# Reordering in the state-space stage: the squares of C on GpSimd, a table load on ScalarE, the mask on VectorE

## The reference, cut to what matters

```python
xp = x @ Wx.T                                    # 64 heads of 8
Bm = rmsnorm((x @ WB.T).reshape(B_, L, H, N), Bn_w) + B_bias      # N = 128 per head
Cm = rmsnorm((x @ WC.T).reshape(B_, L, H, N), Cn_w) + C_bias
dt = softplus(x @ Wdt.T); lam = sigmoid(x @ Wlam.T)
theta_cumsum = cumsum(theta * dt[..., None], axis=1)
Bm, Cm = rope(Bm, theta_cumsum), rope(Cm, theta_cumsum)
alpha = exp(dt * A); beta = (1 - lam) * dt * alpha; gamma = lam * dt
# per token: h = alpha * h + beta * (B_prev x_prev) + gamma * (B x);  y = C . h
```

## Time and profile before

| | us |
|---|---|
| median of three executions | 7745.34 (7743.88 to 7745.35) |
| the profiled execution | 7747.07 |
| its span | 7745.3 |
| mean granted TensorE clock | 0.863 of full |

### The profile page before, as it was taken

The page is one execution under the profiler, slowest core; times in us unless marked ns, Lnnn a source line. Parts: engine busy times, 40 slices in busy tenths (PEclk is TensorE's granted clock), DMA queues, the critical chain, the costliest instruction groups (busy, mean ns, idle before and its releaser), DMA issues. The chain is left out here.

```text
span 7745.3 us, 137299 instructions
## 1 busy us (share of the span) xinstructions
PE 6985.7 (90%) x43387; PEld 5087.3 (66%) x43660; DVE 4741.5 (61%) x8121; ACT 3713.1 (48%) x5855; POOL 3482.4 (45%) x3893
## 2 busy tenths in 40 slices
PE   6999999999684699999999999999999999997499
PEld 4777777777573566666666666666666666666287
DVE  4333333333555477777777777777777777772433
ACT  2222222222222366666666666666666666662111
POOL 0000000000000477777777777777777777771000
PEclk8555555555796899999999999999999999998699
DMA  1000000000101211111111111111111111112100
GB/s 47 4 9 1 4 9 4 9 4 1 57 22 49 89 27 29 28 27 27 28 29 27 30 27 27 29 27 30 27 28 27 27 29 29 29 27 95 53 22 16
DMA packets 388293, 214.26 MB, mean 28 GB/s; under 512 B 248036, under 2 KB 343076, under 8 KB 387140
## 3 DMA queue, kind: packets, MB, share of 16 engines
q1 hardware_dynamic: 379588, 203.05, 10.1%
q10 hardware_dynamic: 8448, 8.39, 0.3%
HBM read 162.02 MB, written 40.64 MB: 26 GB/s over the span
## 5 line engine op out<-in xcount | busy, mean ns | idle before, releaser
L1117 POOL MEMSET ss_rot<- 128x4096 f32 x1 | 3.5, 3511 | 2500.9 <-POOLq L1815 2500.9
L1350 ACT ACTIVATE ss_r<-ss_pssum,ss_eps 128x512 f32<-128x512 f32 x512 | 352.5, 688 | 1131.1 <-PE ss_pssum L1280 1131.1
L1280 PE MATMUL ss_pssum<-ss_sq,ss_pairssum 128*128 128x512 f32 x1024 | 595.4, 664 | 184.0 <-POOL ss_sq L1171 181.2
L1159 POOL TENSOR_TENSOR ss_sq<-ss_sq 128x512 f32<-128x512 f32 x256 | 329.6, 1288 | 914.9 <-ACT ss_sq L1359 914.9
L1409 DVE SCALAR_TENSOR_TENSOR ss_psb<-ss_psb,ss_norm,ss_r 128x512 f32<-128x512 f32 x512 | 362.9, 755 | 510.3 <-ACT ss_r L1352 510.3
L329 PE MATMUL a_ps_o<-a_probt,a_vhead 128*128 128x128 f32 x2560 | 639.7, 414 | 3.6 <-issue 3.5
L329 PEld LDWEIGHTS a_ps_o<-a_probt,a_vhead 128*128 128x128 f32 x2560 | 604.5, 330 | 4.0 <-ACT a_probt L383 1.6
L1261 PE MATMUL ss_psse<-ss_rot 64*128 64x128 f32 x8224 | 530.0, 279 | 0.3 <-POOL ss_rot L1144 0.3
L427 DVE TENSOR_REDUCE a_nmax<-a_ps_p 128x1 f32<-128x384 f32 (+1 forms) x256 | 159.9, 625 | 598.7 <-PE a_ps_p L305 598.7
L1192 POOL TENSOR_TENSOR ss_own<-ident,ss_tk 128x512 f32<-128x512 f32 x512 | 524.9, 1048 | 0.0
L48 PE MATMUL ss_psb<-x_hi,ss_whi 128*128 x1024 | 515.3, 503 | 6.7 <-DVE ss_fr L1397 4.5
(11 more groups left out here) (339 smaller groups left out, 18260.8 us busy)
## 6 DMA issues: line engine op xcount, KB each, us to landing
ss_dtb<-time_steps SPq DMA_DIRECT2D x516, 128.0 KB, 2.9
ss_wraw<-in_w_state SPq DMA_DIRECT2D x264, 80.0 KB, 2.4
ss_xp<-x_heads SPq DMA_DIRECT2D x33, 256.0 KB, 4.4
y_heads<-ss_yo SPq DMA_DIRECT2D x132, 64.0 KB, 2.4
x_heads<-xp_outt SPq DMA_DIRECT2D x32, 256.0 KB, 2.0
ss_right<-decay_rows SPq DMA_DIRECT2D x512, 3.0 KB
ss_left<-decay_rows SPq DMA_DIRECT2D x512, 3.0 KB
op_y<-y_heads SPq DMA_DIRECT2D x8, 1024.0 KB, 6.8
```

The costliest lines, as they stand in the source:

```text
L1159: G.tensor_tensor(sq[:, 0, 0], sq[:, 0, 0], sq[:, 0, 1], ALU.add).then_inc(ss_b, 1)
L1280: M(p_sum[:], pairs_sum[:], sq[:, q, 0], start=True, stop=True).then_inc((sum_b, sum_c)[q], 1)
L1350: A(r[:, q], p_sum[:], ACT.Ln, scale=1.0 / N1, bias=eps[:, 0:1]).then_inc(ln, 1)
```

## The change

Three edits, all inside `state_space`. On GpSimd `decays` takes a second argument; for the units of the loop it now adds the squares of C between its two halves, so L1171 runs behind L1149 and ahead of L1150. On ScalarE the load of the logarithm's set moves from the end of `angles` to behind the Square of B. On VectorE `masked(k)` moves from behind `states` into it, between the copy of the first state (L1421) and the update of the second (L1422); the wait for the copy stands behind the mask. A unit computes with the same instructions as before.

```diff
--- before.py
+++ after.py
@@ -1143,10 +1143,13 @@
                 G.tensor_tensor(rot[:, 1 - j, 2], rot[:, 1 - j, 2], tmp[:, 1, 0], ALU.add)
                 G.tensor_tensor(rot[:, 1 - j, 3], rot[:, 1 - j, 3], tmp[:, 1, 1], ALU.add).then_inc(rot_c, 1)
 
-            def decays(k):
+            def decays(k, squares_c):
                 pool.wait_ge(d_done, k + 1)
                 pool.wait_ge(own_done, k)
                 G.tensor_tensor(dec[:, 0:TPB], dec[:, 0:TPB], own[:, 0:TPB], ALU.add)
+                if squares_c:
+                    pool.wait_ge(sq_c, k + 1)
+                    G.tensor_tensor(sq[:, 1, 0], sq[:, 1, 0], sq[:, 1, 1], ALU.add).then_inc(ss_c, 1)
                 G.tensor_tensor(dec[:, TPB:2 * TPB], dec[:, TPB:2 * TPB], own[:, TPB:2 * TPB], ALU.add).then_inc(dd_done, 1)
 
             with pool.Fori(0, UNITS // 2) as n:
@@ -1165,10 +1168,7 @@
                     G.tensor_tensor(w_lo[:, ds(1 - par, 1), :, ds(b * WCH, WCH)], w_raw[:, j:j + 1],
                                     w_hi[:, ds(1 - par, 1), :, ds(b * WCH, WCH)].bitcast(FP32), ALU.subtract)\
                      .then_inc(w_split, 1)
-                    decays(k)
-
-                    pool.wait_ge(sq_c, k + 1)
-                    G.tensor_tensor(sq[:, 1, 0], sq[:, 1, 0], sq[:, 1, 1], ALU.add).then_inc(ss_c, 1)
+                    decays(k, True)
 
                     pool.wait_ge(pair_in[0], (pair // 2 + 1) * 96)
                     pool.wait_ge(pair_in[1], ((pair + 1) // 2) * 96)
@@ -1194,7 +1194,7 @@
                                                at_diagonal[:, h].broadcast_to([P, TPB, P]), ALU.mult)
                     last.then_inc(own_done, 1)
             turned_c(UNITS, 0)
-            decays(UNITS)
+            decays(UNITS, False)
 
         @block.tensor
         def _(pe):
@@ -1332,7 +1332,6 @@
                 A(trig[:, j, 2], fr[:], ACT.Sin, scale=-UNDER_TURN)
                 act.wait_ge(abs_done, count)
                 A(trig[:, j, 1], trig[:, j, 1], ACT.Sin, bias=quarter[:, 0:1], scale=-UNDER_TURN).then_inc(trig_done, 1)
-                nc.scalar.preload_act_table_set("natural_log_exp_and_others")
 
             def decays(k):
                 act.wait_ge(e_done, k + 1)
@@ -1357,6 +1356,7 @@
                     k = n * 2 + j
                     act.wait_ge(b_done, k + 1)
                     A(sq[:, 0], p_b[:], ACT.Square).then_inc(sq_b, 1)
+                    nc.scalar.preload_act_table_set("natural_log_exp_and_others")
                     decays(k)
                     take_b(k, j, 0)
                     norms(k, 0)
@@ -1418,7 +1418,10 @@
                 sums = p_m[:, 0:6 * PW].rearrange("p (g d) -> p g d", d=PW)
                 link(V.tensor_tensor(sums, sums, blocks[:].rearrange("p (o d) -> p o d", o=1).broadcast_to([P, 6, PW]), ALU.mult))
                 entering = lambda c: state[:, c, :, 0:PW]
-                link(V.tensor_copy(entering(1), added[:, 0]))
+                link.mark(V.tensor_copy(entering(1), added[:, 0]))
+                moved = link.n
+                masked(k)
+                link.wait(moved)
                 link(S(entering(2), entering(1), ends[:, ds(at + 1, 1)], added[:, 1], ALU.mult, ALU.add))
                 S(entering(3), entering(2), ends[:, ds(at + 2, 1)], added[:, 2], ALU.mult, ALU.add).then_inc(s_ready, 1)
 
@@ -1442,13 +1445,11 @@
                     combine(k, j, (older // BATCH) % 2, older % BATCH, link)
                     rotate(k, j, k // BATCH, 0, link)
                     states(k, ends_at(old, 1 - j), link)
-                    masked(k)
                     rotate(k, j, k // BATCH, 1, link)
             assert link.n == PER + 1, link.n
             link = Chain(dve, chain_sem, UNITS * (PER + 1) + first)
             combine(UNITS, 0, 1, BATCH - 2, link)
             states(UNITS, ends_at(LAST, 1), link)
-            masked(UNITS)
             combine(UNITS + 1, 1, 1, BATCH - 1, link)
 
 E1, I1 = 8, 176
```

## The result

The changed kernel takes 7466.12 us (median of four, 7463.08 to 7469.45) against 7745.35: a ratio of 0.964, 95% interval 0.9623 to 0.9656. The span of its profiled execution is 7467.7 us.

What follows compares the result with a forecast made beforehand. The loop through GpSimd's squares of C (L1171) was taken to bound the state-space unit. Removing 181.2 us of TensorE waits and 36.1 us of clock falls, 217.3 us together, from 7745.3 gave 7528 us, range 7500 to 7610.

Steps and rivals of the forecast that it cites:

- The covers: Slack hiding moved work: 0.35 us for ScalarE's table load; VectorE's 0.60 us idle ahead of L1422 for the mask.
- the floor: TensorE's own work in one state-space unit, claimed as 16.22 us, the least a unit could take after the change.
- The 36.1 us: State-space stage: time lost to some 22 falls of TensorE's granted clock to half, all forecast to go.
- The 181.2 us: TensorE's total idle time ahead of L1280, waiting for GpSimd's squares of C (L1171), all forecast to go.
- the sum of 217.3 us: Whole forecast gain in the state-space stage: 181.2 us of waits for L1171 plus 36.1 us of clock falls.
- the first rival: TensorE's clock falls stay although the wait goes: 7564 us with 22 falls, 7600 with 44; chance 0.17.
- The mask edit: Masking between VectorE's state updates, claimed to fill its 0.60 us idle time and be worth 0 within 0.1 us.
- The load on TensorE's path (2): Rival: the moved ScalarE load needs over 1.28 us, delaying the copy of B and C projection: 7766 us; chance 0.05.
- The Square is served by the sine's table (3): Rival claimed the opposite: ScalarE's Square of B needs another load ahead of it, giving 7666 us; chance 0.06.
- VectorE (4): Rival: the 0.60 us ahead of L1422 isn't hidden under the mask, TensorE loses up to 0.4 us: 7630; chance 0.08.
- No change (5): Rival: an unseen wait takes the place of the old one, leaving the time as before; chance 0.03.
- The estimate of 7791 us: Kernel time if the moved ScalarE load also cost the skill page's drain of about 1380 ns, a unit taking 17.25 us.

Runs made afterwards that it cites:

- the last run: The changed kernel with two products of three in the angles' projection and only the first half of the mask computed: 7439.06 us, ratio 0.9601.

## Why the prediction was wrong, point by point

- **The mechanism held.** The loop over GpSimd's squares of C bounded the unit, each of load and order removes that wait, their gains don't add, and TensorE is what is left, in the kernel with all three edits. The covers were found where I named them: 0.30 us behind the moved load, and the mask in the place of the 0.60 us.
- **The step that failed is the floor: "TensorE's own work is thus 16.20 us, 16.22 with the 0.02 us seen at a handover".** It is 15.97 us. Of the 0.25 us, 0.15 us is the end of the chunk sums: I took it from a row's start and length, and the next product starts 0.15 us before it. Nearly all of the other 0.1 us (0.09 us between the rows of one unit, 0.08 us by the run without the load edit) is a wait for L1159, the squares of B, inside the unit that I took as free of waits. I had treated 4392.73 as TensorE's own pace, since no wait was shown on it; the load edit removes this one too. 0.25 us in 255 units are 64 us, and the forecast missed by 62.
- **The falls of the clock.** The 36.1 us are TensorE's extra time at half the clock, and as that they are right: the trace's record of the clock has 22 falls in the stage, 75.1 us together, and half of this is 37.5. But they are not what the falls cost the kernel. A unit with a fall took 17.93 us in the mean, the others 16.99: 22 x 0.94 = 21 us, since the wait at the unit's end shrank from about 0.8 to 0.2 us. The 181.2 us hold the shrunken waits already, so the sum of 217.3 us isn't touched. All falls went, so the first rival fell. Behind the fall at 4347.80 the next wait of the sum for C in the kernel before was 0.25 us (timeline):

```profile
4365.79 1.12 PE L1280 MATMUL ss_pssum<-ss_sq,ss_pairssum 128*128 128x512 f32 x2 [0.25 <-POOL ss_sq L1171]
```

- **The mask edit, "worth 0 within 0.1 us"**, was worth 0.36 us a unit, 94 us. Against a floor of 16.22 us a loop of 16.33 is indeed 0.11 us; against the true floor it is the bound. So the mistake in the floor hid what the edit is for, and a misread row helped: I had the mask without this edit at +17.3, but that is where L1422 starts; the mask stands at 4400.66, which is +17.88, and ends at +19.10. That is behind the factor of the norm of C (+18.76), so without the edit VectorE had no slack there.
- **The rivals.** The load on TensorE's path (2) did not come; brought about with a second load it took 7720 us, under the 7766 that I had for it and under the time before. The Square is served by the sine's table (3): one load stands behind it and none ahead. VectorE (4) loses nothing: the 0.60 us don't show again behind the mask. No change (5) is ruled out by the interval.
- **The page of the Trainium skill**, "ScalarE: Activation LUTs", "What ACT_TABLE_LOAD costs": its 1283 ns are the rows' 1.28 us, here with work waiting on both sides; its 1380 ns of drain show neither at one load nor at two in a row. The estimate of 7791 us by it was not met.

## What to carry to other kernels

Take an engine's floor from start to start across a stretch in which it never stops, not from a start plus a row's length. Where an instruction starts within some 0.15 us of the end of one on another engine that it needs, suspect a wait, whatever the trace names. When a loop is cut, work out every other loop against the new floor: one that had 0.7 us of slack here became the bound, and an edit that is worth nothing alone was worth a third of the whole. Price the edits of a change in all combinations, since load alone gives 188 us and order alone 190 (against 7748.68, the kernel before in their round), both together no more, and all three 279.

## What the runs showed of the hardware

- A product can start before the shown end of the one ahead: 1.36 us behind the start of twelve small products whose row says 1.51. So a wait of 0.12 us can be there with no idle time shown.
- The 0.60 us of idle time ahead of L1422, put down to the copy L1421, can be covered: with 1.23 us of mask in between, the update follows without a gap. It does not look like a wait for the copy's result, since with half a mask (0.69 us, the last run's rows) the update starts 0.94 us behind the copy's end and still 0.09 us behind the mask's. That it is the work on addresses was argued, not shown.
- A wait of TensorE does not by itself bring a fall of the clock. The kernel before waited about 0.8 us a unit and fell from 2.4 to 1.2 GHz in one unit of twelve; the kernel with two loads showed a wait of 0.72 us a unit at another place, and its mean clock was 1.00, with no fall in the record of the stage. What decides is open.
